# Second retention, second experts and last norms as one program instead of three

## The chip, the cores and the metric

The kernel runs on one core of a Trainium2 chip. The metric is the device time of one execution in microseconds (us), the median of three runs. The core has five engines with a queue each: TensorE (PE), VectorE (DVE), ScalarE (ACT), GpSimd (POOL) and SyncE (SP). Every engine works through its own list of instructions in order and waits at semaphores for the others.

## The reference

Two layers on x of 16 sequences x 512 tokens x 128 features, float32. Each layer is an attention part and an expert part, each followed by a layer norm over the sum with its input.

```
x = layernorm(x + retention_0(x))     # 4 heads, rotary, decay, gate
x = layernorm(x + experts_0(x))       # 8 experts, F = 256, best 2 per token
x = layernorm(x + retention_1(x))     # 8 heads of 16, group norm, gate W1, out W2
x = layernorm(x + experts_1(x))       # 8 experts, F = 512, best 2 per token
# experts_1: top_v, top_i = top_k(x @ Wg, 2); w = softmax(top_v)
# y_e = (silu(x @ W1[e]) * (x @ W3[e])) @ W2[e];  out = sum over the 2 of w * y_e
```

Which experts a token takes depends on the data, so the list of work for the expert part is made on the chip.

## The kernel before

It runs five programs one after another: `retention0`, `experts(0)`, `retention1`, `experts(1)`, `finish`. Between two of them stand a barrier of all engines and `clear_semaphores` (L156). The change touches the last three.

**`retention1` (L1322)** works on one sequence per step. A step's body handles seven sequences at different stages, called z, y, a, b, c1, c2, d for lags 0 to 6, so sequence n enters at step n as z and leaves at step n + 6 as d; GpSimd has an eighth stage, e, at lag 7. z loads the results of layer 0, y sums and norms them, a projects q, k and v, b computes scores and outputs, c1 the group norm, c2 the output projection and residual (L1541), d the norm, the router's logits, the choice of two experts (`choose`, L349 on) and the row of each token in its expert's region (`rows_of`). e scatters the rows: `scatter_pair` (L451) sends 8 indirect DMAs of 128 rows to the DRAM tensor `scattered`, which has one region per expert. Steps 0 to 7 are straight code, 8 to 15 a loop of two steps a round, 16 to 21 straight code. From step 18 on a is empty, from step 19 on b too, and so on to step 21, which has d only. After the last step VectorE makes the tile table (`Tiles.table`, L486 to L507): from the number of tokens of each expert, which expert and which first row each of the 71 tiles (`STEPS`) of 256 rows has, in `t_ex` and `t_row`. SyncE fills the rest of each expert's last tile with spare rows (`Tiles.fill`, L478). Then VectorE centres the down weights of all experts at once (`Centered.compute`, L520 to L524).

**`experts(1)` (L1007)** takes the 71 tiles in order. SyncE loads tile n (L1072) two steps ahead. TensorE transposes it (L1226), multiplies gate and up (L1239, 24 matmuls of 256 columns: each product is three, since weights and x are split in a high and a low part) and, two tiles later, down (L1249). ScalarE writes the high parts (L1108, L1111), the silu (L1117), the row indices (L1126) and the weighted results (L1130); VectorE the low parts (L1200, L1204) and gate times up (L1210); GpSimd stores the rows to `expert_out` with two indirect DMAs per tile (L1091). There are four buffers of split weights, split x and h, and two PSUM banks each for transposes, gate, up and down. The first 12 tiles are straight code, then comes a loop of four tiles a round; GpSimd's code is straight throughout.

**`finish` (L1752)** does the last sum and norm, per sequence: SyncE loads both results of its tokens (L1782), VectorE sums (L1809, L1822), ScalarE squares (L276), GpSimd takes the power (L283, L285), VectorE and ScalarE scale half each (L1817, L1838), ScalarE stores (L1844). Five stages at lags 0 to 4.

## Time and profile before

| | us |
|---|---|
| median of 3 runs | 1338.27 (1337.91 to 1346.35) |
| profiled execution, span | 1413.9 |
| PE busy in it | 1150.6 (81%) |
| DVE busy | 910.2 (64%) |
| ACT busy | 716.5 (51%) |
| POOL busy | 742.6 (53%) |
| mean granted TensorE clock | 0.911 |

The profiled execution is one run with the hardware profiler on, and is 75.6 us longer than the median. Clock 1.00 is 2.4 GHz, 0.50 is 1.2 GHz. A timeline row gives start and duration in us, the engine, the line of the kernel, the operation, its output and inputs, how many such instructions are merged (x), and in brackets how long the engine stood idle before it and what ended that. A window row gives the stretch, its length, then for PE, PEld (weight loads), DVE, ACT and POOL the busy time and number of instructions, then clock, share of DMA engines in use, and GB/s.

### The profile page before, as it was taken

What the parts mean: (1) busy time and instruction counts of PE and PEld (TensorE: products, weight loads), DVE (VectorE), ACT (ScalarE), POOL (GpSimd) and SP (SyncE); (2) the same over time, 40 slices, a digit from 0 to 9 for tenths busy, and PEclk for the clock granted to TensorE, in tenths of its full rate; (3) what the DMA queues carried; (4) which work ended last, traced back from release to release, by engine and by line L of the source; (5) the groups of instructions that cost most, each with busy time, mean ns of one, the idle gap of its engine ahead of it and who ended that gap; (6) DMA issues with size and microseconds to landing.
All of it is one profiled execution on the core that took longest, in us unless ns stands there. A gap on an engine that the chain in (4) does not pass through costs nothing. (4 is left out here: it accounts for less than half of the span.)

```text
span 1413.9 us, 33103 instructions
## 1 busy us (share of the span) xinstructions
PE 1150.6 (81%) x10358; PEld 1022.6 (72%) x10359; DVE 910.2 (64%) x2572; ACT 716.5 (51%) x1875; POOL 742.6 (53%) x903
## 2 busy tenths in 40 slices
PE   6999999984188888846899999983599999999930
PEld 5888888863188888844676677662499999999930
DVE  4788888863555555515788887755566666666626
ACT  3344433432255555524566666642466666666627
POOL 0267776765446666651146666666244444444436
PEclk9999999976599999977999999985699999999975
DMA  8121112100322222214222112011211121111138
GB/s 244 44 62 55 39 42 76 32 23 27 101 80 79 82 82 82 83 51 129 76 93 84 57 57 75 30 35 57 60 54 54 53 55 55 54 54 56 39 112 268
DMA packets 75424, 102.22 MB, mean 72 GB/s; under 512 B 15154, under 2 KB 51506, under 8 KB 74866
## 3 DMA queue, kind: packets, MB, share of 16 engines
q1 hardware_dynamic: 49586, 60.96, 15.0%
q0 software_dynamic: 17280, 35.69, 7.7%
q10 hardware_dynamic: 8448, 4.20, 1.0%
q8 instruction: 59, 0.97, 0.3%
q14 instruction: 51, 0.42, 0.1%
HBM read 60.93 MB, written 44.11 MB: 74 GB/s over the span
## 5 line engine op out<-in xcount | busy, mean ns | idle before, releaser
L1091 POOL DMA_INDIRECT expert_out<-e_ysb,e_idx x284 | 306.3, 1078 | 313.7 <-ACT e_ysb L1130 181.7
L1239 PE MATMUL banks<-e_x_hi,e_w_hi 128*128 128x256 f32 x852 | 256.7, 301 | 5.3 <-DVE e_h L1210 3.0
L1239 PE MATMUL banks<-e_x_lo,e_w_hi 128*128 128x256 f32 x852 | 244.3, 287 | 2.0 <-issue 1.8
L1239 PE MATMUL banks<-e_x_hi,e_w_lo 128*128 128x256 f32 x852 | 244.1, 287 | 1.4 <-issue 1.0
L1210 DVE TENSOR_TENSOR e_h<-banks,e_sgl 128x512 f32<-128x512 f32 x213 | 146.8, 690 | 145.6 <-PE banks L1239 84.2
L1249 PE MATMUL banks<-w_dn,e_h 128*128 x1704 | 219.9, 279 | 20.4 <-ACT e_ysb L1135 13.4
L1249 PEld LDWEIGHTS banks<-w_dn,e_h 128*128 128x128 f32 x1704 | 206.4, 195 | 25.1 <-issue 25.1
L1117 ACT ACTIVATE e_sgl<-banks 128x512 f32<-128x512 f32 x213 | 127.9, 600 | 131.0 <-PE banks L1239 84.0
L1239 PEld LDWEIGHTS banks<-e_x_hi,e_w_hi 128*128 128x128 f32 x852 | 166.6, 196 | 8.2 <-issue 8.0
L1239 PEld LDWEIGHTS banks<-e_x_lo,e_w_hi 128*128 128x128 f32 x852 | 166.6, 196 | 3.5 <-issue 3.5
L1239 PEld LDWEIGHTS banks<-e_x_hi,e_w_lo 128*128 128x128 f32 x852 | 166.0, 195 | 0.8 <-issue 0.8
L1200 DVE TENSOR_TENSOR e_w_lo<-w_gu,e_w_hi 128x512 fp32r<-128x512 f32 (+1 forms) x142 | 136.2, 959 | 36.7 <-ACT e_w_hi L1108 26.5
L451 POOL DMA_INDIRECT scattered<-b_r_x,b_r_idx x128 | 130.9, 1022 | 36.2 <-issue 35.9
L451 POOL DMA_INDIRECT scattered<-a_r_x,a_r_idx x128 | 128.5, 1004 | 36.3 <-issue 36.3
L1108 ACT CAST e_w_hi<-w_gu 128x512 fp32r (+1 forms) x142 | 119.7, 843 | 7.0 <-issue 5.3
L1226 PE MATMUL banks<-c_ident,e_xg 128*128 128x128 f32 x284 | 57.4, 285 | 58.4 <-DMA e_xg<-scattered 57.4
L1111 ACT CAST e_x_hi<-banks 128x256 fp32r<-128x256 f32 x142 | 53.4, 376 | 92.9 <-PE banks L1226 58.6
L1531 DVE TENSOR_TENSOR b_sT<-banks,c_causal 128x1024 f32<-128x1024 f32 x64 | 75.4, 1220 | 24.9 <-PE banks L1609 22.1
L1226 PEld LDWEIGHTS banks<-c_ident,e_xg 128*128 128x128 f32 x284 | 36.9, 148 | 60.7 <-issue 52.6
L664 POOL TENSOR_TENSOR a_inv_rms<-a_mse,c_half 128x16 f32<-128x16 f32 x16 | 53.4, 3340 | 46.4 <-DVE a_mse L779 46.4
L1204 DVE TENSOR_TENSOR e_x_lo<-banks,e_x_hi 128x256 fp32r<-128x256 f32 x142 | 59.5, 419 | 23.5 <-ACT e_x_hi L1111 17.4
L901 PEld LDWEIGHTS banks<-a_v,a_sT 128*128 128x128 f32 x512 | 69.4, 197 | 4.0
(280 smaller groups left out, 2463.9 us busy)
## 6 DMA issues: line engine op xcount, KB each, us to landing
e_xg<-scattered SPq DMA_DIRECT2D x142, 130.0 KB, 2.0
b_cy<-expert_out SPq DMA_DIRECT2D x32, 256.0 KB
f_y<-expert_out SPq DMA_DIRECT2D x32, 256.0 KB, 4.4
expert_out<-e_ysb,e_idx POOLq DMA_INDIRECT x284
a_xT<-in_x_T SPq DMA_DIRECT2D x16, 256.0 KB
out<-f_x ACTq DMA_DIRECT2D x16, 256.0 KB, 4.4
scattered<-in_spare SPq DMA_DIRECT2D x2, 1040.0 KB
scattered<-in_spare SPq DMA_DIRECT2D x16, 130.0 KB
```

The source lines that it names most:

```text
L451: nc.gpsimd.indirect_dma_start(out=scattered[0:E * REGION, :], out_offset=bass.IndirectOffsetOnAxis(ap=self.idx[t.odd][:, j:j + 1], axis=0 ...
L901: mm = nc.tensor.matmul(O[:, at + h * DV0:at + (h + 1) * DV0], sT[:, h, c, :], v[b.odd][:, c, h * DV0:(h + 1) * DV0], start=(c == 0 and h ...
L1091: nc.gpsimd.indirect_dma_start(out=expert_out, out_offset=bass.IndirectOffsetOnAxis(ap=idx[d.slot][:, i:i + 1], axis=0), in_=ysb[d.slot][: ...
L1108: nc.scalar.copy(w_hi[b.slot][:], w_gu[:, bass.ds(e, 1), :, 0:F].rearrange("p o g f -> p (o g) f")).then_inc(w_hi_there, 1)
L1117: nc.scalar.activation(sgl[bank_of(j, c)][:], GB[bank_of(j, c)][:].rearrange("p (k n) -> p k n", k=2), ACT.Silu).then_inc(sg_there, 1)
L1200: nc.vector.tensor_tensor(w_lo[b.slot][:], w_gu[:, bass.ds(e, 1), :, 0:F].rearrange("p o g f -> p (o g) f"), w_hi[b.slot][:].bitcast(F32), ...
L1204: nc.vector.tensor_tensor(x_lo[b.slot][:], TP[b.odd][:, 0:ROWS], x_hi[b.slot][:].bitcast(F32), ALU.subtract).then_inc(x_ev, 1)
L1210: nc.vector.tensor_tensor(h[c.slot][:, 2 * j:2 * j + 2, :], UB[bank_of(j, c)][:].rearrange("p (k n) -> p k n", k=2), sgl[bank_of(j, c)][:] ...
L1226: mm = nc.tensor.transpose(TP[b.odd][:, i * P:(i + 1) * P], xg[b.slot][:, i, 0:D], c_ident[:])
L1239: mm = nc.tensor.matmul(banks[bank_of(j, c)][:, i * ROWS:(i + 1) * ROWS], w_[c.slot][:, g, f:f + P], x_[c.slot][:], start=(k == 0), stop=( ...
L1249: mm = nc.tensor.matmul(YB[d.odd][:, i * D:(i + 1) * D], h[d.slot][:, f, i * P:(i + 1) * P], w_dn[:, bass.ds(e, 1), f, :].rearrange("p o d ...
L1531: nc.vector.tensor_tensor(sT[h][:, 2 * g:2 * g + 2, :, :].rearrange("p g n t -> p (g n) t"), pairs[2 + g].rearrange("p g (n t) -> p (g n) ...
```

## The change

`retention1`, `experts(1)` and `finish` become one function, `second_layer`, with one block and no barrier inside.

- All steps are straight code on every engine. The expert work of step u is a `unit(u)`: on TensorE the transposes of tile u, gate and up of tile u - 2, down of tile u - 4; on ScalarE and GpSimd the store side is at u - 5.
- `UNITS` puts 11 units (0 to 10; the change's title says 13 tiles, the code has 11) at places called points 1 to 4 inside steps 18 to 21 of the retention. Units 11 to 76 follow (`STEPS + DRAIN`).
- The tile table is split. `first`, in step 17, lists the 37 tiles (`SURE`) that are certainly full once 11 sequences (`EARLY`) are routed. `second`, after the last step, lists the other 34 from 16 regions: rest of the first 11 sequences, then the rest, for each expert. The number of tiles stays 71.
- Centring is done per expert, two in each of units 0 to 3.
- Split weights, split x and h have three buffers (`RING`) instead of four, laid over retention tiles that are no longer needed, and so are the last norm's. Units below 11 use one bank each for gate, up, transposes and down (PSUM 6, 7, 4, 5); from 11 on they use two. TensorE waits for silu before it writes a gate bank again and for h before an up bank.
- The last norm's rounds (`closing(g)`) 0 to 11 run after units 56, 57, 59, ... 74 (`CLOSING`), when results of the first 11 sequences are complete after tile 50; rounds 12 to 19 follow the last unit. Before load 0 SyncE waits for the stores of 51 tiles, before load 11 for all.
- On ScalarE, in steps from 19 on, the norm's `apply` moves ahead of the group norm's copy.

The diff, cut to its core:

```diff
...
 STEPS = TOKENS * TOPK // ROWS + E - 1
+EARLY = 11
+SURE = (EARLY * T * TOPK - E * (ROWS - 1) + ROWS - 1) // ROWS
+EARLY_STEPS = EARLY * T * TOPK // ROWS + E - 1
...
-        def retention1():
+        class SplitTables:
...
+            def first(self, dve):
...
+                past, past_n = (a[:, 0:SURE * E].rearrange("o (s e) -> o s e", e=E) for a in (self.past, self.past_n))
+                L(nc.vector.memset(self.one[:], 1.0))
+                self.tiles_of(ful, 0)
+                self.tiles_of(self.top_, ROWS - 1)
+                L(nc.vector.tensor_tensor_scan(cum[:], self.one[:, 0:E], ful[:], 0.0, ALU.mult, ALU.add))
...
+                nc.vector.tensor_tensor(past, c_steps[:, k].unsqueeze(2).to_broadcast([1, SURE, E]),
+                                        cum[0:1, :].unsqueeze(1).to_broadcast([1, SURE, E]), ALU.is_ge)
...
+                nc.vector.tensor_reduce(ex, past, AX.X, ALU.add)
+                L(nc.vector.tensor_tensor(past_n, past, ful[0:1, :].unsqueeze(1).to_broadcast([1, SURE, E]), ALU.mult))
...
+                L(nc.vector.tensor_reduce(self.before[:, k], past_n, AX.X, ALU.add))
+                L(nc.vector.tensor_tensor(rowf, c_steps[:, k], self.before[:, k], ALU.subtract))
+                L(nc.vector.tensor_scalar(rowf, rowf, float(ROWS), None, ALU.mult))
+                nc.vector.tensor_copy(t_ex[:, k], exc).then_inc(self.there, 1)
+                nc.vector.scalar_tensor_tensor(t_row[:, k], ex, float(REGION), rowf, ALU.mult, ALU.add).then_inc(self.there, 1)
...
+            def second(self, dve):
...
+                nc.vector.tensor_copy(self.free_i[:], base[0:1, :]).then_inc(self.free, 1)
+                self.tiles_of(self.bot, ROWS - 1)
...
+                nc.vector.tensor_tensor(past, c_steps[:, 0:n].unsqueeze(2).to_broadcast([1, n, 2 * E]),
+                                        self.cum2[0:1, :].unsqueeze(1).to_broadcast([1, n, 2 * E]), ALU.is_ge)
...
+                nc.vector.tensor_reduce(ex, past, AX.X, ALU.add)
+                L(nc.vector.tensor_tensor(past_n, past, w2[0:1, :].unsqueeze(1).to_broadcast([1, n, 2 * E]), ALU.mult))
...
+                L(nc.vector.tensor_reduce(self.before[:, k], past_n, AX.X, ALU.add))
...
+                nc.vector.tensor_scalar(t_ex[:, k], exc, float(E - 1), None, ALU.min).then_inc(self.there, 1)
+                nc.vector.tensor_scalar(t_row[:, k], rowf, first2[0:1, 0:1], None, ALU.add).then_inc(self.there, 1)
...
+        def second_layer():
...
+                UNITS = {(18, 1): 2, (19, 1): 1, (19, 2): 1, (19, 3): 1, (19, 4): 1,
+                         (20, 1): 1, (20, 2): 1, (20, 3): 1, (21, 2): 1, (21, 3): 1}
+                ALONE = sum(UNITS.values())
...
+                def tp_bank(n):
+                    return psum[0] if n >= ALONE and (n - ALONE) % 2 == 0 else psum[4]
...
+                def gate_bank(n, j):
+                    return psum[1] if n >= ALONE and j else psum[6]
+
+                def up_bank(n, j):
+                    return psum[2] if n >= ALONE and j else psum[7]
...
+                DRAIN = 6
+                CLOSED = EARLY
+                CLOSING = {EARLY_STEPS + 5 + 5 * g // 3: g for g in range(CLOSED + 1)}
...
+                    def load_tile(n):
+                        if n == 0:
+                            sp.wait_ge(tables.there, 2)
+                            sp.wait_ge(router.sent[0], SCATTERS * ((EARLY + 1) // 2))
+                            sp.wait_ge(router.sent[1], SCATTERS * (EARLY // 2))
+                        if n == SURE:
+                            sp.wait_ge(tables.there, 4)
+                            sp.wait_ge(tables.filled, 16 * (E + 1))
+                            for i in range(2):
+                                sp.wait_ge(router.sent[i], SCATTERS * SEQS // 2)
+
+                        wait_count(sp, e_x_ev, n - 3)
+                        row = sp.value_load(t_row[0:1, n:n + 1], min_val=0, max_val=E * REGION + (SPARE - E - 1) * ROWS)
+                        sp.dma_start(xg[n % 4][:], scattered[bass.ds(row, ROWS), :].rearrange("(p r) d -> p r d", p=P)
...
+                    def load_results(g):
+                        a = f_turns(g)[0]
+                        if a:
+                            done = EARLY_STEPS if a.n < EARLY else STEPS
+                            if a.n in (0, EARLY):
+                                for i in range(4):
+                                    sp.wait_ge(e_st[i], SENT * ((done + 3 - i) // 4))
...
+                    tables.spare_tiles(sp)
...
+                    for n in range(ALONE + 3):
+                        load_tile(n)
+                    tables.fill(sp)
+                    for u in range(ALONE + 1, STEPS + DRAIN):
+                        if ALONE + 3 <= u + 2 < STEPS:
+                            load_tile(u + 2)
+                        if u in CLOSING:
+                            load_results(CLOSING[u])
+                    for g in range(CLOSED + 1, SEQS + 4):
+                        load_results(g)
...
                                 if e:
                                     router.scatter_pair(pool, e, q)
                             if c2:
                                 norm.power(pool, c2)
+                            fill(1)
                             for q in range(2, 4):
...
+                    for u in range(ALONE, STEPS + DRAIN):
+                        unit(u)
+                        if u in CLOSING:
+                            closing(CLOSING[u])
...
+                                "p o g f -> p (o g) f")).then_inc(e_w_hi_there, 1)
+                            act.wait_ge(e_x_mm, b + 1)
+                            nc.scalar.copy(x_hi[b % RING][:], tp_bank(b)[:, 0:ROWS]).then_inc(e_x_hi_there, 1)
+                        if 0 <= c < STEPS:
...
+                                act.wait_ge(o_mm, SEQS)
...
+                                nc.scalar.activation(sgl[j][:], gate_bank(c, j)[:].rearrange("p (k n) -> p k n", k=2),
+                                                     ACT.Silu).then_inc(e_sg_there, 1)
...
+                            act.wait_ge(e_y_mm, d + 1)
+
+                            wait_count(act, e_st[d % 4], SENT * (d // 4))
...
+                            wait_count(act, router.sent[c2.odd], SCATTERS * c2.half)
+                            wait_count(act, x3_kept, c2.n - 1)
+                            norm.apply(act, r, x3[c2.odd][:, :, 0:D], c2, x3_there)
+                        if not b:
+                            fill(2)
...
+                    def unit(u):
+                        b, c = u, u - 2
+                        if b < STEPS:
...
+                            dve.wait_ge(e_w_hi_there, b + 1)
+                            nc.vector.tensor_tensor(
+                                w_lo[b % RING][:], w_gu[:, bass.ds(e, 1), :, :].rearrange("p o g f -> p (o g) f"),
+                                w_hi[b % RING][:].bitcast(F32), ALU.subtract).then_inc(e_w_there, 1)
+                            dve.wait_ge(e_x_hi_there, b + 1)
+                            nc.vector.tensor_tensor(x_lo[b % RING][:], tp_bank(b)[:, 0:ROWS], x_hi[b % RING][:].bitcast(F32),
+                                                    ALU.subtract).then_inc(e_x_ev, 1)
...
+                            for j in range(PAIRS):
+                                dve.wait_ge(e_u_mm, PAIRS * c + j + 1)
+                                dve.wait_ge(e_sg_there, PAIRS * c + j + 1)
+                                nc.vector.tensor_tensor(h[c % RING][:, 2 * j:2 * j + 2, :],
+                                                        up_bank(c, j)[:].rearrange("p (k n) -> p k n", k=2),
+                                                        sgl[j][:], ALU.mult).then_inc(e_h_there, 1)
+                        if b < E // 2:
+                            centre(2 * b)
+                            centre(2 * b + 1)
+
...
                         if c2 and not b:
                             residual(c2)
+                            fill(1)
...
+                        else:
+                            fill(2)
+                            fill(3)
...
+                        if s == EARLY + 6:
+                            tables.first(dve)
                         if c2 and b:
...
+                        elif b:
+                            fill(1)
...
+                        fill(4)
...
+                    def closing(g):
+                        _, b, _, d, _ = f_turns(g)
+                        if b:
+                            dve.wait_ge(f_got[b.slot], 16 * TOPK * b.quarter + 16 * TOPK)
...
+                            wait_count(dve, f_front_there, b.n - 3)
+                            nc.vector.tensor_tensor(r4[b.slot][:], y4[b.slot][:, 0:CH, :], xres[:, bass.ds(b.n * CH, CH), :],
...
+                        if b:
+                            dve.wait_ge(f_summed, b.n + 1)
+                            nc.vector.tensor_tensor(r4[b.slot][:], r4[b.slot][:], y4[b.slot][:, CH:, :], ALU.add
...
-                    run_steps(dve, first, last, SEQS, lags, body)
-                    tiles.table(dve)
-                    centered.compute(dve)
+                    for s in range(SEQS + 6):
+                        def fill(point):
+                            for u in slot_units(s, point):
+                                unit(u)
+                        step(s, fill)
+                    tables.second(dve)
+                    for u in range(ALONE, STEPS + DRAIN):
+                        unit(u)
+                        if u in CLOSING:
+                            closing(CLOSING[u])
+                    for g in range(CLOSED + 1, SEQS + 4):
+                        closing(g)
...
+                    def unit(u):
+                        b, c, d = u, u - 2, u - 4
+                        if b < STEPS:
...
+                            pe.wait_ge(e_ld[b % 4], b // 4 * 16 + 16)
+                            wait_count(pe, e_x_ev, b if b < ALONE else b - 1)
+                            for i in range(ROWS // P):
+                                mm = nc.tensor.transpose(tp_bank(b)[:, i * P:(i + 1) * P], xg[b % 4][:, i, 0:D], c_ident[:])
...
+                            pe.wait_ge(e_w_there, c + 1)
...
+                            for j in range(PAIRS):
+                                k = PAIRS * c + j if c <= ALONE else PAIRS * c + j - 1
+                                for g, bank_of, freed, done in ((0, gate_bank, e_sg_there, e_g_mm), (1, up_bank, e_h_there, e_u_mm)):
+                                    wait_count(pe, freed, k)
...
+                                        for m, (w_, x_) in enumerate(((w_hi, x_hi), (w_hi, x_lo), (w_lo, x_hi))):
+                                            mm = nc.tensor.matmul(bank_of(c, j)[:, i * ROWS:(i + 1) * ROWS],
...
+                        if 0 <= d < STEPS:
...
+                            pe.wait_ge(e_h_there, PAIRS * d + PAIRS)
+                            wait_count(pe, e_y_there, d if d <= ALONE else d - 1)
...
+                                                          start=(f == 0), stop=(f == FC - 1))
+                            mm.then_inc(e_y_mm, 1)
...
+                        if not b:
+                            fill(2)
...
+                        if not b:
+                            fill(3)
...
+                        if b and not a:
+                            fill(1)
...
```

## Rows read from the trace of the kernel before

**Rows 1.** Windows by stage: us, busy us (count) of five engines, clock, DMA, GB/s

```profile
923.90:940.30 16.40, 13.99 (x173) 10.69 (x169) 11.59 (x45) 7.83 (x24) 10.18 (x19) 1.00 0.09 30
940.30:956.30 16.00, 10.60 (x57) 9.14 (x53) 6.52 (x40) 5.52 (x20) 11.06 (x20) 0.51 0.12 38
956.30:967.50 11.20, 7.11 (x43) 5.94 (x41) 3.51 (x26) 3.54 (x14) 7.74 (x13) 0.65 0.10 32
967.50:978.50 11.00, 3.45 (x27) 2.87 (x24) 2.81 (x25) 3.11 (x8) 6.96 (x13) 0.50 0.11 36
978.50:1005.50 27.00, 0.05 (x2) 0.02 (x1) 14.99 (x27) 2.33 (x2) 16.42 (x18) 0.50 0.28 77
1005.50:1355.80 350.30, 349.39 (x2982) 348.20 (x2982) 225.69 (x426) 223.40 (x493) 149.52 (x138) 0.99 0.19 53
1355.80:1413.90 58.10, 0.00 (x0) 0.00 (x0) 27.09 (x64) 31.05 (x163) 31.64 (x38) 0.54 0.71 224
```

**Rows 2.** Timeline of TensorE, one tile of the second experts

```profile
1103.95 0.38 PE L1226 MATMUL banks<-c_ident,e_xg 128*128 128x128 f32 x2
1104.09 0.36 PE L1239 MATMUL banks<-e_x_hi,e_w_hi 128*128 128x256 f32 x1
...
1107.04 1.95 PE L1249 MATMUL banks<-w_dn,e_h 128*128 x16
1108.82 0.38 PE L1226 MATMUL banks<-c_ident,e_xg 128*128 128x128 f32 x2
```

**Rows 3.** Timeline of VectorE, table and centring at the retention's end

```profile
979.58 0.07 DVE L486 MEMSET b_t_one<- 128x8 f32 x1
...
984.81 4.40 DVE L520 TENSOR_REDUCE b_w_mean<-w_dn 128x32 f32<-128x4096 f32 x1
...
989.61 4.42 DVE L524 TENSOR_TENSOR w_dn<-w_dn,b_w_mean 128x4096 f32<-128x4096 f32 x1
```

**Rows 4.** Groups of instructions by shape, steady part of the second experts

```profile
L1210 DVE TENSOR_TENSOR e_h<-banks,e_sgl 128x512 f32<-128x512 f32 x136 | 93.8, 691 | 61.4 <-PE banks L1239 43.7 <-ACT e_sgl L1117 9.3 <-issue 8.1
L1200 DVE TENSOR_TENSOR e_w_lo<-w_gu,e_w_hi 128x1024 fp32r<-128x1024 f32 x68 | 83.3, 1225 | 33.1 <-ACT e_w_hi L1108 24.9 <-issue 8.1
...
L1204 DVE TENSOR_TENSOR e_x_lo<-banks,e_x_hi 128x256 fp32r<-128x256 f32 x68 | 28.4, 418 | 0.0
```

**Rows 5.** Timeline of GpSimd beside the centring

```profile
988.64 0.96 POOL L451 DMA_INDIRECT scattered<-b_r_x,b_r_idx  x1 [0.30 <-issue]
989.90 4.96 POOL L451 DMA_INDIRECT scattered<-b_r_x,b_r_idx  x1 [0.30 <-issue]
```

**Rows 6.** Timeline of SyncE's queue

```profile
981.56 11.01 SPq L478 DMA_DIRECT2D scattered<-in_spare  x8
```

**Rows 7.** Windows of the second experts: straight code, then the loop

```profile
1024.50:1073.00 48.50, 48.50 (x420) 48.50 (x419) 31.70 (x60) 31.21 (x70) 21.44 (x20) 1.00 0.19 54
1073.00:1341.20 268.20, 268.20 (x2314) 268.20 (x2313) 175.69 (x331) 174.73 (x388) 121.11 (x110) 1.00 0.19 53
```

**Rows 8.** Timeline of ScalarE, SyncE's queue and VectorE at the end

```profile
1358.89 0.19 ACT L1126 CAST e_idx<-e_at 128x2 uint32<-128x2 f32 x1 [4.12 <-DMA c_ident<-in_ident]
...
1367.69 31.48 SPq L1782 DMA_DIRECT2D f_y<-expert_out  x32
...
1371.07 0.69 DVE L1809 TENSOR_TENSOR f_r<-f_y,xres 128x512 f32<-128x512 f32 x1 [19.91 <-DMA f_y<-expert_out]
...
1404.60 0.69 DVE L1809 TENSOR_TENSOR f_r<-f_y,xres 128x512 f32<-128x512 f32 x1
```

**Rows 9.** Timeline of TensorE at the start of the second experts

```profile
1008.38 0.41 PE L1239 MATMUL banks<-e_x_lo,e_w_hi 128*128 128x256 f32 x1
1008.59 0.41 PE L1239 MATMUL banks<-e_x_hi,e_w_lo 128*128 128x256 f32 x1
```

**Rows 10.** Timeline of ScalarE in the first experts

```profile
405.77 0.37 ACT L1111 CAST e_x_hi<-banks 128x256 fp32r<-128x256 f32 x1 [2.39 <-remote]
...
608.50 0.37 ACT L1111 CAST e_x_hi<-banks 128x256 fp32r<-128x256 f32 x1 [2.31 <-remote]
```

422 lines of the change are left out of this document (301 added, 121 removed).

## Prediction

> **What bounds the kernel now.** I read the windows of the profile first, cut at the last matmul of each retention step and at the ends of the stages. Three kinds of stretch show. From 1005.5 to 1355.8 us the second experts run, and TensorE is busy 349.39 of 350.30 us at a granted clock of 0.99: it bounds them, and nothing that only VectorE, ScalarE or GpSimd saves there shortens them [rows 1]. From 940.3 to 1005.5 us lie the last three retention steps and the change of program: TensorE is busy 10.60, 7.11, 3.45 and 0.05 us of 16.0, 11.2, 11.0 and 27.0, at about half clock, and no other engine is full until 978.5 [rows 1]. From 1355.8 to the end at 1413.9 TensorE does nothing [rows 1]. So 65.2 + 58.1 = 123.3 us pass in which the bounding engine of the neighbouring stage is nearly idle. That is what the change works on.
>
> Next the timeline of one steady expert tile on TensorE. Transposes begin at 1103.95, gate and up matmuls at 1104.09, the down matmuls at 1107.04, the next transposes at 1108.82 [rows 2]. A tile is thus T 0.14 + G 2.95 + D 1.78 = 4.87 us; 71 tiles are 345.8, and the stage's 350.3 agree.
>
> **What is removed.** The table of tiles and the centring of the down weights stood alone at the end of the retention: 979.58 to 984.81 for the one, to 994.03 for the other [rows 3]. Then came the last scatters, a barrier and the load of the first tile, until 1005.5. All of that wait goes. The work itself stays and is spread.
>
> **The retention's end, from 940.3 on.** Before: 65.2 us. After, by the engine whose queue I expect to be full in each step:
> - Step 17 gets the first table on VectorE: some 20 small operations and four on 296 elements, where the old table had 568 and took 5.2 us [rows 3]. I estimate 4.6. In front of the operation behind it VectorE is partly idle (a neighbouring step has 16.40 - 11.59 = 4.8 idle, row 1 of [rows 1]). Bounds 0 and 4.6; I take +3.
> - Step 18 gets units 0 and 1. Per unit VectorE splits w (1.23) and x (0.42), with two small copies 1.9 [rows 4], and centres two experts at (4.40 + 4.42 + 0.3)/8 + small = 1.3 each [rows 3]. Behind them on VectorE stand that step's oT and its routing choice, for which TensorE and GpSimd wait, so all is on the path: 2 x 1.9 + 4 x 1.3 = +9.0.
> - Step 19 has units 2 to 5. VectorE: its own 6.5 [rows 1], 4 x 1.9, four tiles of h at 2 x 0.69 = 1.4 [rows 4], four centrings 5.2, together 24.9. It idled 9.5 us of this step; half of that I leave as waits that no unit covers: 30.
> - Step 20 has three units, step 21 two. Here TensorE sets the pace: 7.11 busy at clock 0.65 and 3.45 at 0.50 shrink to about 5 and 1.7 at full clock; 5 + 3 x 4.87 = 19.6 and 1.7 + 2 x 4.87 = 11.4.
> - Then the second table, 34 steps x 16 = 544 elements wide, as the old one, with a few operations more: 6.0. VectorE has it before unit 11, and TensorE can do only T, the gate pair and one up bank of unit 11 in that time (2.3), then waits for split and h (2.6): 6.3.
> Sum 3 + 9.0 + 30 + 19.6 + 11.4 + 6.3 = 79.3, so this part becomes 14.1 longer. Bounds: if only TensorE's work counts, 9 G + 7 D + 11 T = 40.6, plus some 15 of its own and the 6.3, about 62 (-17 against my sum); if units and old steps add up with nothing hidden, 38.2 + 9.0 + 9 x 4.87 + 3 + 6.3 and the idle time that stays, about 105 (+26).
>
> GpSimd gets six tiles' stores in these steps, 12 issues of 0.96 + 0.30 = 15 us [rows 5]. It was the engine with the most work there (11.06, 7.74, 6.96, 16.42) [rows 1], and its last scatters end later by those 15 us. Who waits: tile 37, the first of the second table, 26 tiles of 4.87 later. Cost nothing; if ScalarE's store buffers (four) ran out it would be a few us. One issue took 4.96 instead of 0.96 us beside the 4.42 us centring on VectorE [rows 3, 5]. The Trainium skill (SBUF — State Buffer, "SBUF: two separate sides") explains such a pair: a VectorE operation with two SBUF inputs and a GpSimd operation exclude each other for its whole length. The trace agrees, and by that rule the pieces of 1.1 us cost GpSimd up to 1.1 each where the one piece cost 4.0: about +5 us on GpSimd, where nobody waits, so the sum stays.
>
> SyncE refills the spare rows after the second table; its eight copies took 11.01 us before [rows 6]. Queued behind them is the load of tile 14; tiles 11 to 13 are already in, 3 x 4.87 = 14.6 us of cover plus the 6.3. Cost nothing, 2 us if the cover is gone.
>
> **The experts.** When unit 11 starts, 62 G, 64 D and 60 T are left: 182.9 + 113.9 + 8.4 = 305.2, where the stage took 350.3: -45.1. The loops of 14 rounds become straight code. In the part that was already straight, TensorE is busy 48.50 of 48.50 us, in the loop 268.20 of 268.20 [rows 7]: nothing to gain or lose there. Buffers for split weights fall from four to three; ScalarE writes one after the tile three before is through, which TensorE finishes a whole tile before the value is wanted. Into units 56 to 74 come twelve closing rounds. One norm costs VectorE 27.09/16 = 1.7, ScalarE 31.05/16 = 1.9 and GpSimd about 1.5 us [rows 1]. One round falls on 8.1 us of tiles; VectorE has 225.69 and ScalarE 223.40 of 350.3 in use, 1.7 us free per tile, 2.9 per round. So it is hidden; without that cover 12 x 1.9 = 23.
>
> **The tail.** Before 58.1: 11.9 from TensorE's end to the first load of results (ScalarE's last tile waits 4.12 of it, a barrier ends it), 3.4 to the first sum, 33.5 for fifteen more sums (2.24 each), 9.3 from the last sum to the end [rows 8]. After: no barrier, 9 (bounds 5 and 12); 3.4; four more sums, 9.0; 9.3: 30.7. -27.4.
>
> **Sum.** 14.1 - 45.1 - 27.4 = -58.4, so the profiled execution would go from 1413.9 to 1355.5. The median of the runs shown is 1338.27, 0.9465 of it; the profiled execution is longer throughout, so I scale the gain: 55.3, which gives **1283 us**. Unscaled it would be 1280.
>
> **Rivals.**
> - *Half clock in the last steps.* In the old steps the clock was 0.5 to 0.65 [rows 1]. At half clock a matmul of G starts 0.21 us after the one before [rows 9] instead of 0.12: G 5.1, D 3.4. 9 x 2.2 + 7 x 1.6 = 31 us. For it: units come in single file through one gate and one up bank, with gaps. Against: TensorE would be busy in 70% of the time, more than now. 1283 + 29 = 1312. Chance 0.12.
> - *The units don't overlap the steps.* The part takes 105: 1283 + 24 = 1307. For it: every engine works through one fixed order, so one late reply delays step and unit. Against: VectorE's idle 9.5 in step 19 and TensorE's 4 to 8 in steps 20 and 21 are right at the places of the units. Chance 0.12.
> - *Closing rounds hold TensorE,* for instance when SyncE waits for the 51st tile's stores and the tile loads queue behind: up to 23 us, 1283 + 22 = 1305. Chance 0.06.
> - *Straight code starves an engine.* This ends on the other side. In the first experts, straight on all engines, ScalarE stands still for 2.3 to 5.7 us eleven times between 403 and 609 us with nothing in the profile that it waits for, first and last in [rows 10]. Over 305 us that is 16 times some 3.3 = 53 us: 1283 + 50 = 1333, no change. If VectorE stands apart from that as often, 106 us and 1383. It decides for slower from 21 stops that reach TensorE whole. Against: 48.50 of 48.50 in straight code of the same shape [rows 7]. Chance 0.05 for no change, 0.04 for slower. The Trainium skill (Runtime: NRT & Kernel Launch, "Instruction fetch mechanics") says that sequential code is fetched ahead and that taken branches are what stalls. By that rule this rival is void and the sum holds.
> - *It doesn't do what it says:* the split makes partial tiles twice and more tiles run. The diff leaves STEPS at 71 and the second table's regions begin where the first's end, so no.
>
> **Chances and range.** My forecast 0.61, the three same-signed rivals 0.30, no change 0.05, slower 0.04. Low end: the short bound of the retention's end (-16) and 5 us in the tail give 1263; high end: the half clock's 1312 and a few us of closing rounds. 1260 to 1314 leaves out 0.09 above and some below. The likeliest case alone spans 1265 to 1298. Faster by over 1% (below 1324.9, about what a measurement of this kernel can tell from no change) 0.91, within 1% 0.05, slower 0.04.
>
> **What would show it.** Right: matmuls of units 0 to 10 between about 943 and 1015; a gap of some 6 us on TensorE under the second table; then TensorE full to about 1325 with no gap at units 56 to 74; about 31 us from its last matmul to the end. Wrong: clock near 0.5 under the units; waits of 3 us on ScalarE or VectorE that TensorE repeats; SyncE waiting for stores while tile loads are late; a unit 11 after 1035.

## The result

Medians of 16 executions each: 1332.93 us after, 1343.18 before, ratio 0.9925 (95% interval 0.9907 to 0.9943). That is 0.75% less, within the 1% that counts as no change here, and 50 us above the forecast of 1283. In a later series, in which all executions were longer, the ratio was 0.9974 (0.9951 to 0.9998).

One thing has to be known to read the numbers. The execution of the kernel before that stands ahead of the prediction is some 70 us longer than most in its first retention and first experts, which the change doesn't touch, and hardly in the part that it does: its second retention begins at 633.72 us, in the changed kernel's profile at 561.72. So I compare stages, each from a matmul to a matmul, and times only between kernels run together.

The stages of the changed kernel, as windows: steps 18 to 21 (each from one ranking matmul to the next), then to 1020, the experts to TensorE's last matmul, and the tail.

```profile
core 0: us, PE busy (x) PEld busy (x) DVE busy (x) ACT busy (x) POOL busy (x), PEclk, DMA share, GB/s
852.11:881.39 29.28, 16.96 (x171) 12.61 (x171) 21.07 (x65) 10.05 (x28) 13.53 (x23) 0.79 0.18 51
881.39:924.72 43.33, 33.94 (x187) 31.45 (x188) 24.65 (x76) 15.89 (x39) 12.62 (x22) 0.71 0.09 26
924.72:958.97 34.25, 23.95 (x166) 21.94 (x164) 13.13 (x44) 13.41 (x37) 15.51 (x18) 0.85 0.13 39
958.97:978.96 19.99, 16.88 (x105) 15.88 (x105) 9.07 (x37) 7.97 (x18) 14.45 (x19) 0.74 0.18 51
978.96:1020.00 41.04, 31.62 (x249) 29.89 (x250) 24.52 (x64) 19.10 (x42) 22.74 (x25) 0.96 0.30 80
1020.00:1294.57 274.57, 274.57 (x2394) 274.38 (x2392) 187.66 (x367) 193.23 (x491) 145.03 (x133) 1.00 0.27 81
1294.57:1325.50 30.93, 0.00 (x0) 0.00 (x0) 10.29 (x27) 13.39 (x69) 17.15 (x20) 0.57 0.55 174
```

Against [rows 1] the experts are as full as before and the tail is 30.9 instead of 58.1 us. But steps 18 to 21 take 126.9 us where they took 54.5, and over them no engine is full: TensorE is busy 91.7 us, VectorE 67.9, GpSimd 56.1. The nearest to full is TensorE in step 21, 16.9 of 20.0 us at a granted clock of 0.74.

What a unit there waits for is seen in the chain of waits of the changed kernel (start, duration, engine, what; "issue" is time for which the trace names no cause):

```profile
931.49 0.99 PE banks L2109 x6
...
933.18 0.54 ACT e_ysb L1747 x2
...
933.76 0.73 issue
934.49 1.04 POOL expert_out L1629
...
935.83 0.96 POOL expert_out L1629
...
937.10 0.97 POOL scattered L454
...
938.44 0.97 POOL scattered L454
...
939.71 0.97 POOL scattered L454
940.68 0.30 issue
940.98 2.29 DMA scattered<-b_r_x,b_r_idx
943.27 0.02 issue
943.29 0.28 ACT b_r_x L294
```

The path goes from the gate matmuls to ScalarE's result, through GpSimd's two stores of the tile, four scatters of an earlier sequence that stand behind them, and the landing of the fourth (issued at 940.98), which releases the norm in ScalarE's list; only then come the splits of the next unit. In the waits of steps 18 to 21 (total, times, longest):

```profile
POOL mark L180 <- ACT b_r_th L421: 29.0, 2, 21.8
POOL expert_out L1629 <- ACT e_ysb L1747: 21.1, 5, 8.0
DVE e_w_lo L1912 <- ACT e_w_hi L1726: 20.5, 8, 10.1
...
PE banks L2109 <- ACT e_sgl L1737: 16.4, 6, 6.9
```

So the waits lead from one engine to the next, and each waits for one that is itself held at an earlier place of its list.

### The profile page after: what moved, and what is told of

The parts are those of the page before. It is cut to its first block, busy times and chain, and to the rows that moved or that the text cites. A ratio compares the mean times of both kernels' runs of the same rounds, so it can differ in the third digit from the quotient of the medians.

```text
span 1325.5 us, 31382 instructions
## 1 busy us (share of the span) xinstructions
PE 1134.8 (86%) x10358; PEld 1013.3 (76%) x10358; DVE 915.4 (69%) x2620; ACT 719.6 (54%) x1873; POOL 734.4 (55%) x903
## 4 chain that ended last, share of the span: by engine, by line
PE 31%; DVE 10%; POOL 5%; issue 4%; ACT 4%; DMA 3%; DVEq 0%; ACTq 0%; SPq 0%; POOLq 0%
PE banks L2109 14%; PE banks L2124 9%; DMA scattered<-b_r_x,b_r_idx 2%; DVE b_sT L1868 2%; POOL scattered L454 1%; PE banks L2096 1%; ACT b_cn_sq L279 1%; ACT b_r_x L294 1%; DVE b_cr L1306 1%; POOL b_cn_rstd L288 1%; POOL b_n_rstd L288 1%; PE banks L2036 1%; DVE b_cr L1320 1%; PE banks L2161 1%; POOL b_fn_rstd L288 1%
## 5 line engine op out<-in xcount | busy, mean ns | idle before, releaser
L1629 POOL DMA_INDIRECT expert_out<-e_ysb,b_e_idx x142 | 159.4, 1123 | 168.7 <-ACT e_ysb L1747 139.3
L2109 PE MATMUL banks<-b_e_x_hi,e_w_hi 128*128 128x256 f32 x568 | 172.0, 303 | 26.7 <-ACT e_sgl L1737 16.4
L1094 POOL DMA_INDIRECT expert_out<-e_ysb,e_idx x142 | 138.4, 975 | 69.9 <-issue 38.6
L2109 PE MATMUL banks<-b_e_x_hi,e_w_lo 128*128 128x256 f32 x568 | 163.7, 288 | 0.0
L454 POOL DMA_INDIRECT scattered<-b_r_x,b_r_idx x128 | 129.7, 1013 | 36.1 <-issue 36.1
L2109 PEld LDWEIGHTS banks<-b_e_x_hi,e_w_hi 128*128 128x128 f32 x568 | 111.9, 197 | 30.8 <-ACT e_sgl L1737 18.5
L1912 DVE TENSOR_TENSOR e_w_lo<-w_gu,e_w_hi 128x1024 fp32r<-128x1024 f32 x71 | 87.0, 1225 | 69.1 <-ACT e_w_hi L1726 69.0
L2109 PEld LDWEIGHTS banks<-b_e_x_hi,e_w_lo 128*128 128x128 f32 x568 | 111.3, 196 | 0.0
L1242 PE MATMUL banks<-e_x_hi,e_w_hi 128*128 128x256 f32 x284 | 86.8, 306 | 0.0
L1726 ACT CAST e_w_hi<-w_gu 128x1024 fp32r x71 | 74.1, 1044 | 19.7 <-PE banks L2109 12.2
L1242 PE MATMUL banks<-e_x_hi,e_w_lo 128*128 128x256 f32 x284 | 80.9, 285 | 0.0
```

The lines of the kernel that those rows point to most:

```text
L454: nc.gpsimd.indirect_dma_start(out=scattered[0:E * REGION, :], out_offset=bass.IndirectOffsetOnAxis(ap=self.idx[t.odd][:, j:j + 1], axis=0 ...
L1094: nc.gpsimd.indirect_dma_start(out=expert_out, out_offset=bass.IndirectOffsetOnAxis(ap=idx[d.slot][:, i:i + 1], axis=0), in_=ysb[d.slot][: ...
L1242: mm = nc.tensor.matmul(banks[bank_of(j, c)][:, i * ROWS:(i + 1) * ROWS], w_[c.slot][:, g, f:f + P], x_[c.slot][:], start=(k == 0), stop=( ...
L1629: nc.gpsimd.indirect_dma_start(out=expert_out, out_offset=bass.IndirectOffsetOnAxis(ap=idx[n % 4][:, i:i + 1], axis=0), in_=ysb[n % 4][:, ...
L1726: nc.scalar.copy(w_hi[b % RING][:], w_gu[:, bass.ds(e, 1), :, :].rearrange("p o g f -> p (o g) f")).then_inc(e_w_hi_there, 1)
L1912: nc.vector.tensor_tensor(w_lo[b % RING][:], w_gu[:, bass.ds(e, 1), :, :].rearrange("p o g f -> p (o g) f"), w_hi[b % RING][:].bitcast(F32 ...
```

## The experiments

The table has all runs. Steps go from ranking matmul to ranking matmul; "rest" is from step 21's to TensorE's last matmul; all in us, from one profile each. The first nine and the last eight ran in executions of different length, so the ratio to the kernel before, which ran beside each, compares the times.

| run | steps 18, 19, 20, 21 | sum | rest | median; ratio (interval) |
|---|---|---|---|---|
| e1 before, again | 15.3 16.0 11.2 10.8 | 53.3 | 377.4 | 1344.1, one execution |
| changed | 29.3 43.3 34.3 20.0 | 126.9 | 315.6 | 1332.9; 0.9925 |
| e2 no units | 16.9 21.7 11.9 10.4 | 60.8 | 368.6 | 1320.8; 0.9847 (0.9812 to 0.9882) |
| e3 in a row | 17.4 20.7 11.2 84.5 | 133.8 | 316.7 | 1337.2; 0.9974 (0.9946 to 1.0002) |
| e4 two banks | 27.0 45.0 33.3 14.2 | 119.5 | 310.2 | 1320.1; 0.9832 (0.9772 to 0.9893) |
| e5 no centring | 22.1 40.0 34.5 17.0 | 113.5 | 317.2 | 1321.6; 0.9868 (0.9817 to 0.9919) |
| e6 three buffers | 29.1 45.7 28.6 16.7 | 120.1 | 319.8 | 1317.4; 0.9823 (0.9790 to 0.9855) |
| e7 centring early | 20.8 39.9 34.6 17.0 | 112.3 | 317.2 | 1315.0; 0.9804 (0.9772 to 0.9837) |
| e8 norms after | 26.9 44.9 34.5 17.0 | 123.2 | 317.2 | 1345.8; 1.0036 (1.0001 to 1.0071) |
| e9 none, buffers, early | 17.9 16.0 11.5 6.0 | 51.5 | 363.7 | 1366.5; 0.9656 (0.9627 to 0.9686) |
| e11 four, buffers, early | 17.9 16.1 15.5 17.7 | 67.2 | 353.8 | 1373.4; 0.9696 (0.9662 to 0.9730) |
| e10 eleven, buffers, early, banks | 21.5 40.0 31.1 21.4 | 114.1 | 320.8 | 1389.0; 0.9820 (0.9786 to 0.9855) |
| e12 as e10, late stores | 21.2 41.5 30.7 31.7 | 125.2 | 321.0 | 1400.2; 0.9888 (0.9854 to 0.9922) |
| e13 changed, again | 28.0 45.7 34.6 20.6 | 128.9 | 318.5 | 1402.1; 0.9974 (0.9951 to 0.9998) |
| e14 = e9 | 19.0 15.9 11.2 6.0 | 52.1 | 359.8 | 1359.6; 0.9681 (0.9645 to 0.9717) |
| e15 = e9, split table | 19.1 14.4 11.9 6.0 | 51.4 | 353.4 | 1351.1; 0.9609 (0.9574 to 0.9645) |
| e16 = e10 | 22.4 38.7 31.1 20.8 | 113.0 | 318.3 | 1378.2; 0.9807 (0.9773 to 0.9842) |

The same code in these steps (changed, e8, e13) gives sums of 126.9, 123.2 and 128.9: a difference of 3 us between two single profiles means nothing.

**The kernel before once more.**

> The kernel before, unchanged, profiled once more. The execution shown had its first matmul of the second retention at 633.72 us, the changed kernel at 561.72, though nothing before that point is changed. Theory: those 72 us belong to that one execution and not to the kernel: the first matmul of the second retention now comes at 560 to 564 and the span is about 1341. Rival: the kernel before is truly slower in its first half, and the changed one gains there by a side effect: 630 or more again. A second question is what the second layer alone takes: 780.2 us in the execution shown, 763.8 in the changed kernel; with medians 10 us apart I expect about 774.

Its first matmul of the second retention (instructions of the line, ns, first and last start):

```profile
L1597 PE MATMUL banks<-b_center,b_wvT x2: 421/487/553, 563.4 to 563.7; 128*128 128x128 f32 x2
```

The span was 1342.3, so the second layer took 778.9 us against 780.2 in the execution shown and 763.8 in the changed kernel. The 72 us belong to the execution; the terms of my sum, which all lie in the second layer, were read from rows that hold.

**No units, and units in a row.**

```diff
-UNITS = {(18, 1): 2, (19, 1): 1, ... (21, 3): 1}
+UNITS = {}                # e2
+UNITS = {(21, 4): 11}     # e3
```

> The changed kernel with an empty list of units inside the retention's steps; all 71 tiles come after the second table. Theory A (a unit inside these steps costs more than the 4.87 us of TensorE that it saves later): steps 18 to 21 go from 126.9 back to 54.5 us, the table and the start of the pipeline take about 10, then come 71 tiles at 4.87: TensorE ends about 30 us earlier, 1303 us in all (1300 to 1315). Theory B (the units are hidden in the steps, which are longer for another reason, such as the straight code or the moved norm): the steps stay well above 100 us and 9 gate/up and 7 down tiles, 39 us, come on top: 1355 to 1372.

> The same 11 units with the same single banks, but all at the last place of step 21, one after another, with no retention step between them. It prices a unit by itself. Theory A1 (the chain through one gate and one up bank is what makes a unit cost some 9 us): 54.5 + 11 x 9 = 153 us where the changed kernel has 127, 1359 us in all. Theory A2 (the bank costs little, the 6.1 us of tiles 12 to 14; the rest comes from weaving unit and step through the fixed orders of five engines): 54.5 + 67 + 2 = 124 us, 1330 in all. If a unit alone is as fast as a steady tile: 54.5 + 54 = 108, 1314.

Without units (e2) the kernel is faster than with them, 1320.8 us. Theory A holds in direction, at 12 of the 30 us. The steps give back 66, but the rest grows by 53. The window behind step 21 in the kernel without units:

```profile
919.84:967.01 47.17, 28.17 (x191) 27.05 (x191) 36.62 (x92) 17.57 (x31) 19.96 (x24) 0.70 0.26 70
```

Up to the transposes of tile 7, with the gate and up matmuls of five tiles in it, 47 us pass, and VectorE is busy 36.6 of them: second table, splits and all eight centrings now stand in one row.

The run in a row gives the price of a unit by itself. Its 11 units, between the first transposes of tile 0 and those of tile 11:

```profile
913.95:991.41 77.46, 53.16 (x360) 48.84 (x360) 46.99 (x113) 30.64 (x60) 23.26 (x24) 0.81 0.12 34
```

That is 7.0 us a unit, centring and start of the pipeline in it; the last of them come at 6.1, the pitch of the single banks. Theory A1 (9 us through the single bank) falls, and so does a unit at 4.87. Woven into the steps the same 11 units add 126.9 - 53.3 = 73.6 us to the steps of before. **Against those, weaving hides 4 of 77 us.** Against the run in a row itself, whose plain steps are a little longer than before (step 19 is 20.7 instead of 16.0), it hides 133.8 - 126.9 = 7; against e2 it would be 11. By any of the three it is far from the 32 of the forecast.

**Two banks for the second pair.**

```diff
-return psum[1] if n >= ALONE and j else psum[6]
+return psum[1] if n >= 4 and j else psum[6]
...
-k = PAIRS * c + j if c <= ALONE else PAIRS * c + j - 1
+k = PAIRS * c + j if c <= 4 else PAIRS * c + j - 1
```

(up likewise, in bank 3)

> From tile 4 on, whose gate and up matmuls come in step 20, the second pair of a tile has banks of its own (1 and 3, free since step 19). Theory A1 (the single bank makes the unit cost 9 us): tiles 4 to 10 fall to about 5, 7 x 4 = 28 us less, 1305. Theory A2 (weaving): only the three tiles of 6.1 us after the table fall to 4.87, 4 us, and up to as much in steps 20 and 21: 1325 to 1329. If neither holds, 1333 as before.

Steps 18 to 20 stay (105.3 against 106.9), step 21 is 14.2 and the rest 310.2 instead of 315.6. Tiles 12 and 13, behind the table, follow after 5.9 and 7.1 us instead of 12.0 and 6.1, since TensorE has a second pair of banks to go on with. So the bank costs mostly where tiles follow each other, as A2 says, and not inside steps 18 to 20. In step 21 some 3 us may be the bank's: with single banks it took 20.0 here, but 17.0 in e5, e7 and e8. The median is lower than A2's range, but with an interval of 16 us.

**Centring left out, and moved.**

```diff
-if b < E // 2:
-    centre(2 * b)
-    centre(2 * b + 1)
```

and in the third run, at the end of VectorE's step:

```diff
+if 9 <= s < 9 + E:
+    centre(s - 9)
```

> The changed kernel without the centring of the down weights in units 0 to 3 and without TensorE's wait for it: that part of the computation is left out, so this only prices it. In the changed kernel's chain of waits the centring stands from 869.8 to 878.7 and from 905.3 to 909.4 us. Theory C (it is on the path that the steps and TensorE wait for): steps 18 and 19 get 10 to 13 us shorter, 1320 to 1323 us. Rival (GpSimd's scatters or the silu chain would have filled that time anyway): at most 3 us, 1330 or more.

> The same centring, one expert at the end of each of steps 9 to 16, where VectorE is busy 15.2 of about 18 us, nothing left out. If theory C holds and VectorE's idle time in those steps takes the 1.6 us of one expert: 1320 to 1324 us, like without centring. If VectorE sets those steps too, they get 1.6 us longer each and the gain is given back: 1333. If both centring places are free, 1333 as well, but with steps 9 to 16 unchanged.

Steps 18 and 19 together: 62.1 and 60.7 us instead of 72.6 (71.8 and 73.7 in e8 and e13). Theory C holds: centring was on the path with about 11 us. Done early it costs some 0.5 us a step, as e14 shows: 17.5 to 17.6 us for steps 7 to 9, 18.0 for most after them, where e6 has 17.5 throughout.

**A third buffer for the scattered rows.**

```diff
-self.x = [[sb(..., [P, CH, WIDE]) for i in range(2)] for k in range(TOPK)]
+# three, used by t.n % 3, with three indices and three semaphores
-wait_count(act, router.sent[c2.odd], SCATTERS * c2.half)
+if c2.n >= 3: act.wait_ge(router.sent[c2.n % 3], SCATTERS * (c2.n // 3))
```

> The rows that the router scatters, and their indices, get a third buffer, so that ScalarE's norm waits for the scatters of three sequences before instead of two. Theory S (in steps 19 and 20 the landing of GpSimd's scatters, with two expert stores in front of them, holds ScalarE and through its fixed order the units behind): ScalarE's waits of 1.47 and 3.80 us for the landing go, and with them 5 to 10 us of steps 19 to 21: 1323 to 1328 us. The steps of 23 instead of 18 us that are now and then seen before step 18 should go as well (up to 5 us more). Rival: GpSimd's own issues, eight of 1.26 us a sequence, set the pace and one more buffer doesn't change it: within 2 us of 1333.

Steps 7 to 16 as one window, first of the changed kernel, then with three buffers:

```profile
649.64:831.95 182.31, 173.84 (x1851) 129.89 (x1851) 151.80 (x559) 118.63 (x381) 118.61 (x209) 1.00 0.21 63
```

```profile
648.55:823.79 175.24, 171.62 (x1850) 129.69 (x1850) 151.16 (x559) 118.44 (x381) 119.36 (x209) 1.00 0.21 65
```

Every one of these steps is now 17.5 us, TensorE busy 171.6 of 175.2. In the changed kernel ScalarE had waited for scatters in nine of these ten steps:

```profile
ACT b_r_x L294 <- DMA scattered<-b_r_x,b_r_idx: 14.6, 9, 2.1
```

With three buffers the line is gone. Single steps of 21 to 24 us, at no fixed place, are in the profiles of e1 to e5, e7 and e13, and in none of the eight with three buffers (19.0 at most). Their length is TensorE's clock. Three steps of e2, the second of them long:

```profile
683.81:701.94 18.13, 17.41 (x186) 13.00 (x186) 15.19 (x56) 11.85 (x39) 11.94 (x22) 1.00 0.21 65
701.94:725.19 23.25, 22.11 (x185) 16.44 (x186) 15.19 (x56) 11.98 (x39) 13.02 (x23) 0.78 0.17 49
725.19:742.72 17.53, 17.16 (x185) 12.97 (x186) 15.03 (x56) 11.97 (x39) 10.74 (x20) 1.00 0.20 59
```

The granted clock is 0.78 to 0.92 in every one of these long steps and 1.00 in all other steps 7 to 16 of all profiles, while e2's longest wait for a landing in them is 2.6 us. TensorE was busy 17.41 of 18.13 us in the step before the clock fell. Why it fell there no run shows; the changed kernel and e8 have the same waits and no such step.

In the change's own steps the third buffer saves some 5.7 us of step 20 (28.6 against 34.3 to 34.6) and nothing sure elsewhere. It has a price behind them: in all eight kernels with three buffers a tile of the experts takes 4.87 us, in the changed kernel and the others without it 4.82, which is 2.8 us over 60 tiles (rest 319.8 against 315.6 in all); why was not tried. Theory S holds, and most of its gain lies in steps that the change leaves alone.

**The last norms behind the experts.**

```diff
-CLOSED = EARLY
+CLOSED = -1
```

> All 20 rounds of the last norm come after the last unit, none inside the experts. My account of the tail (2.24 us a sum, twelve rounds hidden under the tiles): twelve rounds x 2.24 = 27 us more after TensorE's last matmul, nothing less before it: 1360 us. If the rounds inside the experts cost TensorE or the transfers something, the tail still grows by 27 but TensorE ends earlier by that amount, so less than 1350.

The tail:

```profile
1291.41:1335.60 44.19, 0.00 (x1) 0.00 (x0) 23.88 (x59) 31.15 (x163) 31.75 (x37) 0.53 0.74 237
```

44.2 us, where 27 + 30.9 = 58 was expected; and nothing earlier gets shorter (rest 317.2). The sums have the pitch of before (10 in 22.8 us), so the twelve rounds are worth only 13.3 us. The other 13 come from something that I had not put down as a gain: the first 11 sequences need only the first 51 tiles, so their loads no longer wait for the last stores, and VectorE's first sum comes at 1286.70, 4.7 us before TensorE's end, where in e1 it came 14.1 after it. The missing barrier is in these 13 as well; no run separates the two.

**All together.** e9 has no units, three buffers and early centring; e10 the 11 units besides, with two banks; e11 only tiles 0 to 3, in steps 20 and 21; e12 is e10 with

```diff
-for u in slot_units(s, point):
+for u in {(21, 1): range(9), (21, 2): [9], (21, 3): [10]}.get((s, point), []):
```

on GpSimd.

> Three changes at once on the changed kernel: no units inside the retention's steps, three row buffers, centring in steps 9 to 16. If the stages add up as the single runs show them (562 to the second retention, 281 to step 17 with three buffers, 54 for steps 18 to 21 without units, some 8 for second table and first tiles, 345 for 71 tiles, 31 for the tail): 1283 us. If VectorE can't take the centring inside steps of 17.5 us (15.2 + 1.6 + waits), 8 us more: 1291. If a unit in the steps is worth something once centring and landing are out of the way, this run is slower than the next one.

> The same buffers and centring, and the 11 units in their old places with two banks from tile 4 on. Steps 18 to 21 took 126.9; less 14.6 by the centring (measured), 6.8 by the third buffer (measured), 7.4 by the banks (measured): about 98, and 310 to TensorE's end: 562 + 281 + 98 + 310 + 31 = 1282 plus 2, 1284 us. That is 4.0 us per unit, a little less than the 4.87 that a unit saves. If the three savings are one and the same wait, they don't add up and it is 1292 or more.

> As the run without units, but tiles 0 to 3 in steps 20 and 21: four transposes and the gate and up matmuls of two tiles, no down matmuls and no stores. In those steps TensorE is busy 3.3 of 10.4 us and VectorE 2.8. Theory: these parts cost about 2 us a step and save two G (5.9), four T and the filling of the pipeline (3): 4 to 7 us less than without units, 1278 us. Rival: every unit costs what it saves wherever it stands: the same time as without units within 2 us.

> As the run with 11 units, three buffers and two banks, but GpSimd's stores of tiles 0 to 3 leave steps 19 and 20 and go to one place in step 21, behind the first scatters of sequence 14. Theory P (GpSimd's fixed order, 10.1 us of scatters a sequence and 2.5 us for each tile's stores, sets step 20): step 20 gets 5 to 8 us shorter, step 21 up to 3 longer, 1280 us. Rival (TensorE's, ScalarE's and VectorE's fixed orders set it): within 2 us of the run with 11 units.

The kernel before took 1415 us in this series, so the expected times don't apply, but the order does: 1366.5 without units, 1373.4 with four, 1389.0 with eleven. Four units cost 15.7 us in the steps and save 9.9 in the rest.

In e10 the three savings don't add up to the 98 us that I expected: the steps are 114.1 and the rest is 320.8, where e4 had 310.2. Centring's share is there (61.5 us for steps 18 and 19), and 3.2 of the buffer's 5.7 in step 20. For step 21 and the rest the comparison with e4 isn't a clean one. In this series and the next, ScalarE and VectorE stand still in step 21 or the first tiles for 1.7 to 6.6 us at a time with nothing in the trace that releases them: counting those over 1.5 us, five such stops in e10 and in e12, four in e16 and in e15, two in e14, one in e9 and in e11, none in e13, in the changed kernel's first profile and in e1 to e8. In e16, the same kernel as e10:

```profile
1023.72 0.69 DVE L1937 TENSOR_TENSOR e_h<-banks,e_sgl 128x512 f32<-128x512 f32 x1 [4.85 <-DMA a_w_raw<-in_w_proj]
...
1041.23 0.60 ACT L1750 ACTIVATE e_sgl<-banks 128x512 f32<-128x512 f32 x1 [3.32 <-remote]
...
1046.92 0.69 DVE L1937 TENSOR_TENSOR e_h<-banks,e_sgl 128x512 f32<-128x512 f32 x1 [6.63 <-DMA a_w_raw<-in_w_proj]
```

The load a_w_raw is one of layer 0, long landed, so it is no cause. ScalarE's silu was ready at 1020.05 and 1041.83, so VectorE stood 3.7 and 5.1 us; in e4 it starts the same operation 0.1 us after the silu. In e10 such stops make some 4 to 5 us of step 21 (my estimate): without them it would be about 17, as in e5, e7 and e8, still above the 14.2 of e4. From the transposes of tile 11 to those of tile 16 e4 takes 30.6 us, e10 38.6 and e16 36.1; these 8.0 and 5.5 us, where the stops lie, and the 2.8 of the tile's 4.87 make up the difference in the rest (10.6 and 8.1). So e10 doesn't show that the savings are one and the same wait.

Theory P falls: without the stores GpSimd is busy 10.0 of 30.7 us in step 20, with them 15.4 of 31.1 (e16), and the step is as long either way. Step 21 is 10 us longer in e12, but stops of 6.5, 5.0 and 3.6 us stand in it too, so the share of the stores is open.

**Side by side, and the table split.** e15 puts the four pieces of the second table behind units 6 to 9 and one spare row block in each unit from 12 on.

> The changed kernel itself, unaltered, beside the next three on one chip. The executions of the kernel before took 1336 to 1347 us on two chips and 1411 to 1418 on a third, so times of different calls can't be subtracted. If the chip changes only the stages that the change leaves alone (first retention, first experts), the distance of this kernel to the one before is 8 to 15 us wherever it runs.

> The kernel without units, with three row buffers and centring in steps 9 to 16, once more, beside the one with 11 units. Theory W (weaving a unit into a step hides nothing, the unit costs at least what it costs alone): this one is 15 to 25 us faster than with 11 units on this chip too, and 45 to 55 faster than the changed kernel. Rival (the 22 us between them came from that one chip's slower transfers): the two are within 4 us, as the sum of the single savings had it.

> The 11 units with three row buffers, early centring and two banks, beside the kernel without units. Theory W: 15 to 25 us slower than that. Rival: within 4 us of it. In either case faster than the changed kernel by 18 to 30 us, the three single savings together.

> As the one without units, with the second table cut into four pieces on VectorE behind units 5 to 9 and SyncE's refill of the spare rows cut into eight pieces, one a unit from unit 12 on. In the trace of the kernel without units TensorE waits 6.49 us under the table and 3.65 for tile 3's load, which stands behind the refill. If VectorE's free time of a tile (1.7 us) and two tiles of lead take the pieces: 8 to 10 us faster than the kernel without units. If the pieces only move the wait: within 2 us.

The changed kernel is 4.3 us faster than the one before in this series, less than the 8 to 15 that I expected. Theory W holds in its order and its first number: 1359.6 without units against 1378.2 with eleven and 1402.1 for the changed kernel, all run together (42.5 us apart, where I had 45 to 55). Steps 18 to 21 and the first tiles, without units:

```profile
911.09:930.09 19.00, 16.51 (x166) 12.16 (x167) 11.71 (x45) 7.48 (x25) 11.22 (x21) 0.85 0.18 50
930.09:945.97 15.88, 10.50 (x51) 9.04 (x51) 6.49 (x40) 5.52 (x20) 11.05 (x19) 0.52 0.13 42
945.97:957.19 11.22, 7.13 (x38) 5.86 (x38) 3.50 (x26) 4.27 (x16) 7.95 (x13) 0.65 0.09 30
957.19:963.23 6.04, 3.17 (x20) 2.71 (x21) 2.81 (x25) 1.83 (x4) 3.94 (x9) 0.50 0.15 47
963.23:993.63 30.40, 21.01 (x148) 19.77 (x149) 21.97 (x62) 14.17 (x24) 18.87 (x22) 0.75 0.35 95
```

and with eleven:

```profile
913.75:936.15 22.40, 16.92 (x170) 12.57 (x171) 15.04 (x53) 10.21 (x28) 13.78 (x24) 0.86 0.23 63
936.15:974.87 38.72, 29.32 (x186) 27.50 (x187) 18.81 (x64) 15.72 (x39) 13.15 (x21) 0.82 0.11 32
974.87:1005.98 31.11, 24.14 (x167) 22.60 (x164) 12.99 (x44) 13.32 (x37) 15.42 (x17) 0.84 0.14 41
1005.98:1026.80 20.82, 13.58 (x105) 12.99 (x105) 8.79 (x37) 8.10 (x19) 15.19 (x24) 0.89 0.18 52
```

The steps grow by 60.9 us, the rest shrinks by 41.5. A unit costs 5.5 in the steps and saves 3.8 behind them. Of the 19.4 us between these two sums the stops without a releaser make up a part: some 3.7 in step 21, and 5.5 less 1.7 in the first tiles. That leaves about 12, my estimate from these rows. Steps 19 to 21 with nothing woven in run at 0.50 to 0.65 of the clock with every engine partly idle, and that is still cheaper.

Splitting the table gives another 8.5 us, as expected. The waits that it removes, as TensorE has them in e9:

```profile
979.87 0.66 PE L2109 MATMUL banks<-c_ident,b_e_xg 128*128 128x128 f32 x2 [6.49 <-issue]
989.05 0.69 PE L2109 MATMUL banks<-c_ident,b_e_xg 128*128 128x128 f32 x2 [3.65 <-DMA b_e_xg<-scattered]
```

**The best version** is e15: the one program, the split table and the closing rounds of the change, without its units, with three row buffers and early centring: 1351.1 us where the kernel before took 1406.4 and the changed one 1402.1. In the executions of the usual length it was not run.

## Why the prediction was wrong

- **What bounds which stage:** right. The experts stay full and the idle stretches are where they were.
- **Step 17, the first table:** 20.2 us; the kernel before, profiled again, has 18.4. +1.7, I took +3.
- **Steps 18 to 21: the step that failed.** I had 25.4 + 30 + 19.6 + 11.4 = 86.4, measured 126.9. The sum held that 11 units add 31.9 us to the old steps, though alone, at 4.87 and with 10.4 of centring, they would take 64.0: so it let 32 us overlap with idle time. The run in a row corrects both numbers. The units alone take 77.5, not 64, and 4 of it overlaps, not 32: 13.5 + 28 = 41.5 us, the 40.5 that were missing and a little. Half of VectorE's idle time in step 19, and TensorE's pace in steps 20 and 21, took an engine's idle total as room for work. No engine was full; in the chain of waits one reply after another passes through the fixed lists of four engines. That the units don't overlap is shown by the runs; that the order of the lists is the reason is read from the chain, and shown only for three of its waits (e4, e6, e7).
- **Terms taken as nothing there:** the third buffer is worth 5.7 us in step 20, so GpSimd's scatters and stores were not free ("who waits: tile 37") - ScalarE's norm waits for their landing. The single banks make a tile in a row 6.1 instead of 4.87 us; I had the banks in the description of the change and not in the sum.
- **Centring:** taken as 10.4, measured about 11. Right.
- **Second table:** 6.3 taken. Tile 12's transposes come 12.05 us after tile 11's, 7.2 over the pitch.
- **Experts:** from unit 11's transposes to TensorE's end 314.1 us, expected 6.3 + 305.2 = 311.5. Single banks, still in use until unit 15, make two tiles of 6.1 and two of 5.9 us, 4.5 more; the full pitch is 4.82, not 4.87, 3 less. Straight code, three buffers and twelve closing rounds cost nothing: 274.57 of 274.57.
- **Tail:** 30.9, expected 30.7, and right piece by piece: 13.3 to the first sum (12.4), 8.4 for four more (9.0), 9.2 from there (9.3). What I hadn't seen is that the rounds under the tiles are worth only 13.3 of the 27 us; with the rounds behind the tiles e8 still saves the other 13.
- **Scaling** of the gain by 0.9465 had no ground: the second layer takes 780.2 and 778.9 us in a long and a usual execution. It moved the forecast by 3 us. The median before of 1338.27 that I started from became 1343.18 with more executions, 5 us more.
- **The outcome:** no change had a chance of 0.05, for straight code. That rival names 1333, the time that was measured, but this is luck: it lost its 50 us in the experts, where none was lost.

Rivals. *Units don't overlap the steps* is what happened; I gave it 0.12 and priced it at 4.87 a unit, so its 1307 was too low as well. *Half clock* is a part: TensorE is busy 91.7 us in steps 18 to 21 against 34.6, 57.1 more, for work of 9 G + 7 D + 11 T = 40.6 at full clock, so some 16.5 us by the granted clock of 0.71 to 0.85, half of the 31 that I priced (the old steps had 1.00, 0.51, 0.65 and 0.50 in e1); how much of that is on the path is open. *Closing rounds* is void, TensorE 274.57 of 274.57. *Straight code* is void for this result: ScalarE and VectorE have no stop over 1.5 us without a releaser in the second layer of the changed kernel's profile. In the longer executions there are such stops, but none behind the first few tiles. (The Trainium skill, Runtime: NRT & Kernel Launch, "Instruction fetch mechanics", has sequential code fetched ahead; this trace agrees, TensorE 274.57 of 274.57.) My mark for being wrong, a unit 11 after 1035, was met: 980.46 plus the 72 us between the executions is 1052.

What stays open: which of the fixed lists would have to be reordered so that a unit overlaps, what the three savings give together without the stops, and what these stops are.

## What to carry to other kernels

Idle time of an engine inside steps that are bound by waits is not by itself room for work: with fixed lists on five engines the woven work added nearly its full length here. Where it may be hidden is a gap that the same engine would wait through, with nothing urgent behind it; no run here has tried such a place. Price woven work first alone and in its own buffers (a run with all of it in one row costs one line), then claim overlap only for single waits found in the timeline. And look at a recurrent wait of 1 to 2 us in the steady steps before rebuilding their end: the third buffer took 7 us from ten plain steps. Before two runs are compared, see whether both have the same stops that no engine caused: some 12 us of my comparison of e10 with e4 lie at such stops.
